# A two-layer transformer block on one core: the triangular inverse's lowest level in compact buffers on four quadrants, and the first layer's slot in a new order

## The chip, the cores and the metric

One Trainium2 chip, one of its cores. The metric is the device time of one launch in microseconds (us), median of three runs.

## The reference

`x` is (8, 256, 128) in float32. Four blocks are added to it in turn, each on a layer norm of `x`:

```python
x = x + L0_attn(_layernorm(x))   # gated delta rule, 16 heads, key 64, value 128
x = x + L0_ffn(_layernorm(x))    # x @ sign(weight).T
x = x + L1_attn(_layernorm(x))   # causal softmax attention, 16 heads of 8, 4 KV heads
x = x + L1_ffn(_layernorm(x))    # mixture of 8 experts, top 2
```

The change is in the first of them. q, k and v are projected, put through a causal convolution of four taps and silu, q and k are scaled to length one, and for each head

```python
def step(S, inp):
    q_t, k_t, v_t, a_t, b_t = inp
    kS = einsum('bhd,bhdv->bhv', k_t, S)
    kkS = einsum('bhd,bhv->bhdv', k_t, kS)
    S = a_t * (S - b_t * kkS) + einsum('bhd,bhv->bhdv', k_t, v_t)
    return (S, einsum('bhdv,bhd->bhv', S, q_t))
```

runs over 256 time steps. Its outputs are divided by their root mean square and projected.

## The kernel before

The recurrence is done in chunks of 128 time steps: within a chunk a unit triangular matrix of 128 x 128 has to be inverted, and the rest is matmuls. The work is cut into 32 units `n` (4 pairs of batch rows, 8 pairs of heads each: `NP`, `NG`); a unit has 8 half-chunk blocks of 64 x 64 to invert (`NJ`).

All engines run one loop over slots `s`, written out by hand for each engine. In slot `s` the unit `g = s - 9` is at its Gram matrices and masks, `i = g - 1` at the start of its inverse, `j = g - 2` at the inverse's end and the solves, `w = g - 3` at its output. An engine runs what stands in its list in that order, and waits on semaphores; a late operation holds up all that stands behind it on its engine. `s` goes from 9 to 43; k and q projections for units ahead run in slots up to 31, and items of the second layer stand in the last slots. The second layer then has a loop of its own ("ticks").

What a unit goes through, in the order of its data:

- `kproj`, `kcopy`, `kconv`, `ksilu`, `ksq`, `ksel` and `vproj`, `vcopy`, `vconv`, `vsilu`, `vtr`, `vV`: projections on TensorE, copies and silu on ScalarE. A convolution's three taps are each a `scalar_tensor_tensor` on VectorE (L1463), each waiting for the tap before. There are twelve taps in a slot.
- `gram(n, 0..2)` on TensorE (L719) fills banks 3 and 1; ScalarE's `exp` makes the decay masks from exponents that SP loads from DRAM (`exponents`, L469) and GpSimd makes causal (`causal`, L1896); VectorE's `am(n, 0..5)` (L1532, L1535) multiplies the two into `AM`. GpSimd's `scaled` (L1888) makes the scaled keys that `gram` needs, from factors that SP spreads (`spread`, L480).
- `blocks(n)` on SP, released by `am(n, 5)`: four DMAs write the diagonal 32-blocks of `AM` to DRAM (L489), four read them back into `SU` with one row of matrix per partition range (L495).
- `substitute(n)` on GpSimd (L1872 to L1880): forward substitution inside 16 x 16 blocks, a memset and 28 dependent steps over the free dimension.
- `inv_0` on VectorE: turns `SU` (L1546), spreads it on the diagonal of `YP` (L1548), transposes into `XP` (L1553). Then level 0 joins 16-blocks to 32-blocks: `inv_a` (L746), `inv_p` (L1557), `inv_b` (L757), `inv_y` (L1563, L1566), on 64 x 64 tiles. Level 1 joins 32 to 64 by the same functions, and `inv_c`, `inv_n`, `inv_d`, `inv_o` join 64 to 128.
- `solve1`, `u1`, `solve2`, `solve3`, `u2`, `out`, `ot`, `squares`, `rms`, `wout`: solves, output, root mean square and the output projection, which VectorE adds into `X` (L1595).

At the change of each group of 8 units come `lengths` and `gates` (per-head scalars; SP moves them to DRAM by `factors`), and in fixed slots a layer norm or the sign-weight matmul of a finished part. `fill` are matmuls without use that keep TensorE busy.

## Time and profile before

| | us |
|---|---|
| median of 3 runs | 1286.54 (1285.4 to 1288.22) |
| the profiled execution | 1296.63 |
| its span, first to last instruction | 1294.8 |
| TensorE busy | 1147.9 (89%) |
| VectorE busy | 925.0 (71%) |
| ScalarE busy | 814.3 (63%) |
| GpSimd busy | 644.5 (50%) |

"Busy" is the union of an engine's instructions. In the rows a line is start, duration, engine, line of the kernel, operation, output<-inputs, shapes and count; in brackets the idle time ahead of it and what ended it. A float32 matmul shows as two records, with a weight load (PEld) for each. On SP only DMA issues show, and what stands there is the time that issuing took. The chain that ended last runs over TensorE for 60% of the span. A part of this chain says which engine worked at each moment; it does not say which order would have been faster.

### The profile page before, as it was taken

What the parts mean: (1) busy time and instruction counts of PE and PEld (TensorE: products, weight loads), DVE (VectorE), ACT (ScalarE), POOL (GpSimd) and SP (SyncE); (2) the same over time, 40 slices, a digit from 0 to 9 for tenths busy, and PEclk for the clock granted to TensorE, in tenths of its full rate; (3) what the DMA queues carried; (4) which work ended last, traced back from release to release, by engine and by line L of the source; (5) the groups of instructions that cost most, each with busy time, mean ns of one, the idle gap of its engine ahead of it and who ended that gap; (6) DMA issues with size and microseconds to landing.
All of it is one profiled execution on the core that took longest, in us unless ns stands there. A gap on an engine that the chain in (4) does not pass through costs nothing.

```text
span 1294.8 us, 32678 instructions
## 1 busy us (share of the span) xinstructions
PE 1147.9 (89%) x12540; PEld 842.7 (65%) x12540; DVE 925.0 (71%) x1785; ACT 814.3 (63%) x1462; POOL 644.5 (50%) x1192
## 2 busy tenths in 40 slices
PE   5779999999999999989999999998779887898991
PEld 1123677777767777767777777776555454798991
DVE  4757689988899989889976787776556658152232
ACT  5876787887888787898785666765243433333330
POOL 1015667767667776767774766674220102204314
PEclk9879699999999999999997999999889998899996
DMA  4012332221221122112212222240101011488982
GB/s 150 1 60 70 113 84 54 53 71 52 51 69 48 53 52 73 45 53 54 69 25 74 65 68 53 58 67 15 28 7 33 18 19 68 153 282 299 319 301 55
DMA packets 130106, 106.18 MB, mean 82 GB/s; under 512 B 59472, under 2 KB 116816, under 8 KB 129696
## 3 DMA queue, kind: packets, MB, share of 16 engines
q1 hardware_dynamic: 127904, 99.90, 27.1%
q0 software_dynamic: 2048, 4.20, 1.0%
q8 instruction: 100, 1.64, 0.5%
q14 instruction: 54, 0.44, 0.1%
HBM read 84.21 MB, written 15.73 MB: 77 GB/s over the span
## 4 chain that ended last, share of the span: by engine, by line
PE 60%; DVE 16%; issue 7%; ACT 7%; POOL 5%; DMA 2%; SPq 1%; POOLq 0%; DVEq 0%; ACTq 0%
PE pair L719 8%; PE bank L1015 6%; PE bank L757 4%; PE pair L683 3%; PE bank L1022 3%; PE bank L969 3%; PE bank L746 3%; PE pair L651 3%; PE bank L771 3%; PE bank L764 3%; DVE vc L1463 2%; PE bank L815 2%; PE bank L799 2%; PE bank L842 2%; DVE kc L1463 2%
## 5 line engine op out<-in xcount | busy, mean ns | idle before, releaser
L1880 POOL TENSOR_TENSOR SU<-SU 128x28 f32<-128x28 f32 (+6 forms) x448 | 197.4, 441 | 35.1
L1876 POOL TENSOR_TENSOR SU<-SU 128x28 f32<-128x28 f32 (+6 forms) x448 | 194.0, 433 | 35.3
L1463 DVE SCALAR_TENSOR_TENSOR vc<-vy,conv,vc 128x512 f32<-128x512 f32 x192 | 144.5, 753 | 6.0 <-ACT vc L1160 1.5
L1463 DVE SCALAR_TENSOR_TENSOR kc<-ky,conv,kc 128x512 f32<-128x512 f32 x162 | 127.0, 795 | 7.6 <-ACT kc L1134 5.1
L1776 DVE TENSOR_TENSOR vy<-bank,vc 128x512 f32<-128x512 f32 x46 | 31.8, 692 | 98.9 <-PE bank L1015 97.6
L719 PE MATMUL pair<-SM,KQ 64*128 64x128 f32 (+1 forms) x512 | 77.3, 380 | 23.0 <-DVE AM L1532 20.4
L1941 POOL TENSOR_TENSOR RR<-RR,nh 128x8 f32<-128x8 f32 x32 | 57.1, 1785 | 75.3 <-DVE RR L1583 72.3
L1855 POOL TENSOR_TENSOR st<-st,nh 128x4 f32<-128x4 f32 x16 | 16.6, 1040 | 146.8 <-DVE st L1439 110.1
L651 PE MATMUL pair<-xnT,WQ 128*128 128x512 f32 x128 | 76.3, 681 | 5.9 <-ACT qb L1134 5.1
L757 PEld LDWEIGHTS bank<-YP,PP 64*64 64x64 f32 x2048 | 66.6, 138 | 17.1 <-issue 12.7
L1532 DVE TENSOR_TENSOR AM<-pair,SM 128x512 f32<-128x512 f32 x76 | 48.9, 685 | 38.1 <-PE pair L719 34.9
L746 PE MATMUL bank<-XP,AM 64*64 64x32 f32 x2048 | 71.8, 220 | 2.5 <-DVE XP L1566 1.2
L757 PE MATMUL bank<-YP,PP 64*64 64x32 f32 x2048 | 73.8, 223 | 0.1
L683 PE MATMUL pair<-xnT,WQ 128*128 128x512 f32 x128 | 72.3, 648 | 1.0 <-DVE SM L1482 1.0
L1872 POOL MEMSET SU<- 128x32 f32 x32 | 5.0, 156 | 137.0 <-DMA SU<-scratch 137.0
L746 PEld LDWEIGHTS bank<-XP,AM 64*64 64x64 f32 x2048 | 64.7, 134 | 12.2 <-issue 6.4
L719 PEld LDWEIGHTS pair<-SM,KQ 64*128 64x128 f32 x512 | 40.8, 194 | 47.0 <-DVE AM L1532 40.1
L1015 PE MATMUL bank<-YF,AM 128*128 128x128 f32 x512 | 68.0, 279 | 0.0
L719 PE MATMUL pair<-KQ 64*128 64x128 f32 (+1 forms) x512 | 67.3, 341 | 0.0
L1888 POOL TENSOR_TENSOR SM<-KQ,SM 128x512 f32<-128x512 f32 x32 | 44.1, 1377 | 44.1 <-DMA SM<-fscr 44.1
L1929 POOL DMA_INDIRECT SU<-ys,PP x32 | 30.3, 948 | 71.5 <-DMA ys<-YF 60.3
L1546 DVE STREAM_TRANSPOSE PP<-SU 128x512 f32<-128x512 f32 x32 | 35.0, 1093 | 41.8 <-PE bank L771 40.6
(307 smaller groups left out, 3118.7 us busy)
## 6 DMA issues: line engine op xcount, KB each, us to landing
AM<-in_wex_dram SPq DMA_DIRECT2D x32, 768.0 KB, 5.1
SM<-dscr SPq DMA_DIRECT2D x58, 256.0 KB, 3.7
V<-in_wex_dram SPq DMA_DIRECT2D x14, 768.0 KB, 5.5
et<-dscr SPq DMA_DIRECT2D x38, 256.0 KB, 3.7
SM<-fscr SPq DMA_DIRECT2D x64, 128.0 KB, 2.9
scratch<-AM SPq DMA_DIRECT2D x128, 48.0 KB, 1.8
SU<-scratch SPq DMA_DIRECT2D x128, 32.0 KB
xs<-idle SPq DMA_DIRECT2D x2, 1472.0 KB, 9.7
```

The costliest lines, as they stand in the source:

```text
L651: e.matmul(kbank(t)[:, :], wqkv[:, ct * 128:(ct + 1) * 128], xT[:, p % 3, :], start=True, stop=True).then_inc(s_kproj, 1)
L683: e.matmul(vbank(v)[:, :], wqkv[:, ct * 128:(ct + 1) * 128], xT[:, (n // NG) % 3, :], start=True, stop=True).then_inc(s_vproj, 1)
L719: ins = e.matmul(bank[(3, 1)[hh]][:, part], KQ[hp:hp + 64, m, b, 0, s0:s0 + 128], moved, start=True, stop=True)
L746: ins = e.matmul(half(bank[4][pq, j * 64:j * 64 + 64], lv, 0), block_of(n, j, q, 64 * q), half(XP[pq, j, :], lv, 0), start=True, stop=True)
L757: ins = e.matmul(half(bank[5][pq, j * 64:j * 64 + 64], lv, 1), PP[pq, j, :], half(YP[pq, j, :], lv, 1), start=True, stop=True)
L1015: ins = e.matmul(bank[4 if kind == "G" else 6][:, jj * 128:(jj + 1) * 128], W[:, o + jj * 128:o + jj * 128 + 128], XST[i % 2], start=True, ...
L1463: e.scalar_tensor_tensor(c, y[:, :, k:k + 256], conv[:, ct, k:k + 1], c, ALU.mult, ALU.add).then_inc(s_c, 1)
L1532: ins = e.tensor_tensor(AM[:, hh, part, :].rearrange("p (c n) -> p c n", c=3)[:, 0:3:2, :], G[:, :].rearrange("p (k t) -> p k t", k=2), E. ...
L1876: e.tensor_tensor(tmp[:, :, 0:k, 0:15 - k], sub[:, :, 0:k, k:k + 1].to_broadcast([128, 2, k, 15 - k]), sub[:, :, k:k + 1, k + 1:16].to_bro ...
L1880: e.tensor_tensor(sub[:, :, 0:k, k + 1:16], sub[:, :, 0:k, k + 1:16], tmp[:, :, 0:k, 0:15 - k], ALU.subtract).then_inc(s_su, 1)
L1888: e.tensor_tensor(KT2[:, n % 2], KQ[:, n % RK, :, 0, :], FB[:, n % 2, :].rearrange("p (b t) -> p b t", b=2), ALU.mult).then_inc(s_kt, 1)
L1941: e.tensor_tensor(RR[:, 1, :, :], RR[:, 0, :, :], nh[:, :].rearrange("p (t h) -> p t h", t=4), ALU.pow).then_inc(s_r2, 1)
```

## The change

- **Compact level 0.** New buffers `Y0`, `X0`, `PP0` (8 x 32 per partition). Level 0 works on 32 x 32 tiles at the four diagonal positions: `inv_a0`, `inv_b0` have 32 matmuls each with 16 columns, where 16 matmuls had 64 x 64 weights and 32 columns. VectorE's `inv_turn`, `inv_y0`, `inv_x0`, `inv_p0`, `inv_s0` handle half or a quarter of the elements; a new `inv_w0` widens `Y0` into `YP`, and `inv_x1` transposes that.
- **Substitution on 64 partitions.** `SU` shrinks from 1056 to 512 columns. The two 16-blocks that lay side by side in a partition now lie in partitions 8 apart, so each GpSimd step has half the elements. `blocks` reads back with eight DMAs of half the size, where there were four. The `SU` read-back waits for the turn of the unit before, which now stands before `am(4)`.
- **Taps of two tiles apart.** Each parity of k and v tiles has its own tap semaphore, and other work stands between a tile's taps.
- **A new order of the slot** on all engines. `exp` of unit `g + 1` runs at the end of slot `g`; `causal(g + 1)` moves to the head of GpSimd's slot; level 1's `inv_a1` moves to the end of the slot before; `rms` is cut in two. At the change of a group SP sends exponents' factors first, and `key_factors` and `spread` stand behind `blocks`.
- `inv_n` writes `XP`, `inv_c` writes bank 5; some `fill` and some semaphores go; the second layer's `GB` moves from `SU` into `V`.

```diff
-        SU = sb("SU", [128, 1056])
+        SU = sb("SU", [128, 512])
+        su2 = SU[:, :].rearrange("p (r x t) -> p r x t", r=16, x=2)
+        sub, tmp = su2[:, :, 0, :], su2[:, :, 1, :]
...
                 if n:
-                    e.wait_ge(s_tt, n)
+                    e.wait_ge(s_i0, 3 * n - 2)
                 for a in range(4):
                     e.wait_ge(s_bo[a], 16 * n + 16)
-                    e.dma_start(SU[32 * a:32 * a + 8, 0:1024], scratch[a].rearrange("(m c) r t -> m c (r t)", c=3)[:, 0:2, :]).then_inc(s_bi, 16)
+                    rows = scratch[a].rearrange("(m c) r t -> m c (r t)", c=3)
+                    for h in range(2):
+                        e.dma_start(SU[32 * a + 8 * h:32 * a + 8 * h + 8, 0:496], rows[:, 0:2, 528 * h:528 * h + 496]).then_inc(s_bi, 16)
...
             for n in range(NN):
-                if n and n + 1 < NN: spread(n + 1)
+                new = (n + 1) % NG == 0
+                if n and n + 1 < NN and not new: spread(n + 1)
                 if n + 1 < NN: exponents(n + 1)
                 blocks(n)
+                if n + 1 < NN and new:
+                    key_factors((n + 1) // NG)
+                    spread(n + 1)
...
+            def inv_a0(n):
+                if n:
+                    e.wait_ge(s_ip, 2 * n)
+                e.wait_ge(s_ix, 2 * n + 1)
+                for j in range(NJ):
+                    for a in range(4):
+                        r = slice(32 * a, 32 * a + 32)
+                        ins = e.matmul(bank[4][r, 16 * j:16 * j + 16], N4(n)[r, j // 2, j % 2, r], X0[r, j, 0:16], start=True, stop=True)
+                ins.then_inc(s_ia, 1)
...
+            def inv_turn(n):
+                if n:
+                    e.wait_ge(s_ib, 2 * n)
+                e.wait_ge(s_su, NSU * n + NSU)
+                e.transpose(flat(PP[:, :, :]).rearrange("p (t m) -> p t m", t=16),
+                            sub.rearrange("p r t -> p t r").unsqueeze(2).to_broadcast([128, 16, 2, 16])).then_inc(s_i0, 1)
...
-                    e.tensor_tensor(tmp[:, :, 0:k, 0:15 - k], sub[:, :, 0:k, k:k + 1].to_broadcast([128, 2, k, 15 - k]),
-                                    sub[:, :, k:k + 1, k + 1:16].to_broadcast([128, 2, k, 15 - k]), ALU.mult).then_inc(s_su, 1)
+                    e.tensor_tensor(tmp[:, 0:k, 0:15 - k], sub[:, 0:k, k:k + 1].to_broadcast([128, k, 15 - k]),
+                                    sub[:, k:k + 1, k + 1:16].to_broadcast([128, k, 15 - k]), ALU.mult).then_inc(s_su, 1)
...
                 if w >= 0:
...
                 if gap(s + 1, "norm") is not None:
                     norm(gap(s + 1, "norm"))
-                if g + 1 < NN: causal(g + 1)
                 if g < NN: substitute(g)
```

The order on VectorE in the middle of a slot with gates, before (L1546 is the turn of `SU`; L1535 is `am(4)` and `am(5)`; L1463 are taps):

```order
L1463 SCALAR_TENSOR_TENSOR kc<-ky,conv,kc 128x512 [waits s_kconv]
L1532 TENSOR_TENSOR AM<-pair,SM 128x2x256 [waits s_gk,s_exp] x2
L1563 TENSOR_TENSOR YP<-YP,bank 128x8x32 [waits s_ib]
L1569 STREAM_TRANSPOSE XP<-YP 32x8x32 [waits s_iy]
L1579 STREAM_TRANSPOSE ST<-bank 128x256 [waits s_ms]
L1583 SCALAR_TENSOR_TENSOR RR<-ST,QN 128x8 [waits s_r2,s_mt]
L1535 TENSOR_TENSOR AM<-pair,et 128x2x256 [waits s_gk,s_exp] x2
L1463 SCALAR_TENSOR_TENSOR kc<-ky,conv,kc 128x512 [waits s_kconv]
L1481 TENSOR_SCALAR SM<-pair,SM 80x512 [waits s_gab]
L1482 COPY SM<-pair 16x512
L1546 STREAM_TRANSPOSE PP<-SU 128x512 [waits s_su,s_yfc,s_yfd]
L1548 TENSOR_TENSOR YP<-PP,bmask 128x512 [waits s_tt]
```

and after (L1573 is the turn, L1564 are `am(4)` and `am(5)`, L1578 and L1584 `inv_y0` and `inv_x0`):

```order
L1627 STREAM_TRANSPOSE ST<-bank 128x256 [waits s_ms]
L1491 SCALAR_TENSOR_TENSOR vc<-vy,conv,vc 128x512 [waits s_vconv0]
L1561 TENSOR_TENSOR AM<-pair,SM 128x2x256 [waits s_gk,s_exp] x2
L1491 SCALAR_TENSOR_TENSOR vc<-vy,conv,vc 128x512 [waits s_vconv0]
L1573 STREAM_TRANSPOSE PP<-SU 128x512 [waits s_su,s_ib]
L1564 TENSOR_TENSOR AM<-pair,et 128x2x256 [waits s_gk,s_exp]
L1578 TENSOR_TENSOR Y<-PP,bmask 128x256 [waits s_i0]
L1564 TENSOR_TENSOR AM<-pair,et 128x2x256 [waits s_gk,s_exp]
L1584 STREAM_TRANSPOSE X<-Y 128x256 [waits s_i0]
L1633 SCALAR_TENSOR_TENSOR RR<-ST,QN 128x8 [waits s_r2,s_mt]
L1491 SCALAR_TENSOR_TENSOR vc<-vy,conv,vc 128x512 [waits s_vtap,s_vcopy]
L1588 TENSOR_SCALAR PP<-bank,bmask 128x8x16 [waits s_ia]
```

The turn stood behind the last `am` and now stands before its last two.

The order on SP at the change of a group, before (L446 and L448 are `factors`, L480 `spread`, L469 `exponents`, L489 and L495 `blocks`):

```order
L446 DMA dscr<-SM 16x512 [waits s_gs]
L448 DMA fscr<-SM 16x512 [waits s_fr]
L480 DMA SM<-fscr 64x512 [waits s_kt,s_fw]
L480 DMA SM<-fscr 64x512
L469 DMA et<-dscr 128x2x256 [waits s_mk,s_am,s_fw]
L469 DMA SM<-dscr 128x2x256 [waits s_mk,s_am]
L469 DMA SM<-dscr 128x4x128 [waits s_mk,s_am]
L489 DMA scratch<-AM 32x12x32 [waits s_bi,s_am]
L489 DMA scratch<-AM 32x12x32 x3
L495 DMA SU<-scratch 8x1x1024 [waits s_bo0,s_tt]
L495 DMA SU<-scratch 8x1x1024 [waits s_bo1]
```

and after (L453 is `key_factors`, L485 `spread`, L494 and L502 `blocks`):

```order
L494 DMA scratch<-AM 32x12x32 [waits s_bi,s_am]
L494 DMA scratch<-AM 32x12x32 x3
L502 DMA SU<-scratch 8x1x496 [waits s_bo0,s_i0]
L502 DMA SU<-scratch 8x1x496
L502 DMA SU<-scratch 8x1x496 [waits s_bo1]
L502 DMA SU<-scratch 8x1x496
L502 DMA SU<-scratch 8x1x496 [waits s_bo2]
L502 DMA SU<-scratch 8x1x496
L502 DMA SU<-scratch 8x1x496 [waits s_bo3]
L502 DMA SU<-scratch 8x1x496
L453 DMA fscr<-SM 16x512 [waits s_fr]
L485 DMA SM<-fscr 64x512 [waits s_kt,s_fw]
```

`spread` stood ahead of `exponents` and `blocks`, and now stands behind both; `blocks` has eight reads.

The order on TensorE around level 0, before (L746 is `inv_a`, L651 `kproj`, L791 and L799 `solve2` and `solve3`, L842 `wout`):

```order
L791 MATMUL bank<-U,AM 128x128 [waits s_u1]
L791 MATMUL bank<-U,AM 128x128 x3
L746 MATMUL bank<-XP,AM 64x2x16 [waits s_ix,s_x]
L746 MATMUL bank<-XP,AM 64x2x16 x15
L651 MATMUL pair<-xnT,WQ 128x512 [waits s_vtap]
L799 MATMUL bank<-V,YF 128x128 [waits s_v2]
```

and after (L756 and L764 are `inv_a0` and `inv_b0`, L665 `kproj`, L819 `solve2`):

```order
L756 MATMUL bank<-X,AM 32x16 [waits s_ix,s_ip]
L756 MATMUL bank<-X,AM 32x16 x31
L819 MATMUL bank<-U,AM 128x128 [waits s_u1]
L819 MATMUL bank<-U,AM 128x128 x3
L665 MATMUL pair<-xnT,WQ 128x512 [waits s_vtap]
L764 MATMUL bank<-Y,PP 32x16 [waits s_ip]
L764 MATMUL bank<-Y,PP 32x16 x31
```

Level 0 has twice the matmuls at a quarter of the area, and its first group stands before `solve2`.

## Rows read from the trace of the kernel before

**Rows 1.** The page, busy time and granted clock in 40 slices.

```profile
PE 1147.9 (89%) x12540; PEld 842.7 (65%) x12540; DVE 925.0 (71%) x1785; ACT 814.3 (63%) x1462; POOL 644.5 (50%) x1192
...
PEclk9879699999999999999997999999889998899996
```

**Rows 2.** Busy us of PE, PEld, DVE, ACT, POOL by stretch; PEclk, DMA.

```profile
166.80:674.70 507.90, 489.49 (x5632) 371.35 (x5632) 464.47 (x842) 419.26 (x748) 360.43 (x678) 0.99 0.21 55
674.70:705.70 31.00, 30.25 (x294) 23.91 (x290) 17.82 (x34) 16.62 (x30) 16.04 (x37) 0.78 0.27 72
705.70:873.20 167.50, 155.03 (x1920) 124.50 (x1918) 131.83 (x266) 113.01 (x207) 115.43 (x243) 1.00 0.27 62
...
679.40:693.00 13.60, 13.60 (x102) 10.03 (x100) 6.82 (x13) 4.70 (x10) 4.30 (x6) 0.50 0.37 92
```

**Rows 3.** Timeline of TensorE, start and duration in us, two slots.

```profile
471.23 0.49 PE L719 MATMUL pair<-SM,KQ 64*128 64x256 f32 x2
...
498.53 0.70 PE L719 MATMUL pair<-SM,KQ 64*128 64x256 f32 x4
...
501.16 0.70 PE L719 MATMUL pair<-SM,KQ 64*128 64x256 f32 x4 [0.90 <-DVE AM L1532]
...
503.27 0.64 PE L826 MATMUL bank<-qb,ones 128*32 128x256 f32 x8
...
513.89 1.12 PE L746 MATMUL bank<-XP,AM 64*64 64x32 f32 x32
514.95 1.12 PE L651 MATMUL pair<-xnT,WQ 128*128 128x512 f32 x2
...
523.14 0.70 PE L719 MATMUL pair<-SM,KQ 64*128 64x256 f32 x4
```

**Rows 4.** Timeline of VectorE in the same slot.

```profile
505.12 1.29 DVE L1535 TENSOR_TENSOR AM<-pair,SM 128x512 f32<-128x512 f32 x2
...
508.24 1.11 DVE L1546 STREAM_TRANSPOSE PP<-SU 128x512 f32<-128x512 f32 x1 [1.17 <-PE bank L771]
509.39 1.06 DVE L1548 TENSOR_TENSOR YP<-PP,bmask 128x512 f32<-128x512 f32 x1
510.48 0.71 DVE L1553 STREAM_TRANSPOSE XP<-YP 128x512 f32<-128x512 f32 x1
...
512.12 2.32 DVE L1463 SCALAR_TENSOR_TENSOR vc<-vy,conv,vc 128x512 f32<-128x512 f32 x3
...
515.06 0.69 DVE L1557 TENSOR_TENSOR PP<-bank,lmask 128x512 f32<-128x512 f32 x1
...
526.23 0.74 DVE L1463 SCALAR_TENSOR_TENSOR kc<-ky,conv,kc 128x512 f32<-128x512 f32 x1
```

**Rows 5.** Timeline of GpSimd, one substitution.

```profile
514.05 0.16 POOL L1872 MEMSET SU<- 128x32 f32 x1 [4.55 <-DMA SU<-scratch]
514.29 0.25 POOL L1876 TENSOR_TENSOR SU<-SU 128x28 f32<-128x28 f32 x1
...
521.90 0.76 POOL L1880 TENSOR_TENSOR SU<-SU 128x112 f32<-128x112 f32 x1
...
523.54 0.42 POOL L1880 TENSOR_TENSOR SU<-SU 128x112 f32<-128x112 f32 x1
...
529.12 0.23 POOL L1880 TENSOR_TENSOR SU<-SU 128x28 f32<-128x28 f32 x1
```

**Rows 6.** Timeline of SP, DMA issues of the same unit.

```profile
506.44 1.87 SPq L489 DMA_DIRECT2D scratch<-AM  x4
509.38 2.65 SPq L495 DMA_DIRECT2D SU<-scratch  x4
```

**Rows 7.** Timeline of GpSimd, a substitution in a slot without k taps.

```profile
769.41 0.15 POOL L1872 MEMSET SU<- 128x32 f32 x1 [4.69 <-DMA SU<-scratch]
...
782.29 0.23 POOL L1880 TENSOR_TENSOR SU<-SU 128x28 f32<-128x28 f32 x1
```

**Rows 8.** The page, DMA issues: count, KB each, median us to landing.

```profile
SM<-fscr SPq DMA_DIRECT2D x64, 128.0 KB, 2.9
```

More of the change, by code:

```diff
@@ L238, in wide @@
             return b[:, :].rearrange("p (j n) -> p j n", j=NJ)
-        def mask(lv, q):
-            return lmask[q, lv:lv + 1, :].to_broadcast([q.stop - q.start, NJ, 64])
         def N4(n):
@@ L569, in _ @@
             exponents(0)
+            key_factors(0)
             spread(0)
@@ L1062, in _ @@
                 if has_g: gram(g, 0)
+                if has_g: vproj(2 * g)
                 if gap(s, "lengths") is not None: lengths(gap(s, "lengths"))
@@ L1100, in _ @@
                 more(s, 7)
-                if has_w and has_g: wout(w, 1)
-                elif w < 0: fill(2)
-                if has_i: inv_b(i, 0)
+                if has_w: wout(w, 0)
+                if has_w: wout(w, 1)
+                elif w < 0: fill(4)
+                for it in PREP0.get(s, []): prep(*it)
                 if has_j: out(j, 0)
@@ L1106, in _ @@
                 more(s, 8)
-                if has_j: out(j, 1)
-                if has_g: vtr(2 * g)
+                if has_i: inv_a1(i)
+                if has_j and j >= NN - 3: out(j, 1)
                 more(s, 9)
@@ L1279, in _ @@
             e.activation(sgn[:, :], sgn[:, :], ACT.Sign).then_inc(s_sgn, 1)
-            e.wait_ge(s_zero, 3)
+            e.wait_ge(s_zero, 4)
+            for i in range(3):
+                exp(0, i)
             def item(kind, *a):
@@ L1374, in _ @@
-                more(s, 1)
-                if 0 < g < NN: vV(2 * g - 1)
-                if has_g: exp(g, 2)
-                if gap(s, "norm") is not None: norm(gap(s, "norm"))
-                more(s, 2)
-                more(s, 3)
-                if has_k: ksilu(2 * s)
+                has_n = 0 <= g and g + 1 < NN
+                if s % NG == 3 and 1 <= s // NG < NP: gates1(s // NG)
+                if has_l: lengths1(p)
+                if s % NG == 4 and 1 <= s // NG < NP: gates2(s // NG)
@@ L1389, in _ @@
-                if has_k: ksq(2 * s + 1)
-                if has_g: vcopy(2 * g)
+                more(s, 0)
+                if has_k: ksq(2 * s)
+                if has_g: vcopy(2 * g)
+                if gap(s, "norm") is not None: norm(gap(s, "norm"))
+                if has_j: inv_yf(j)
+                more(s, 1)
+                more(s, 2)
+                if has_j: inv_n(j)
+                more(s, 3)
+                if has_k: ksilu(2 * s + 1)
+                if has_k: ksq(2 * s + 1)
```

342 lines of the change are left out of this document (183 added, 159 removed).

## Prediction

> **What bounds the kernel now.** I read the busy shares and slices first, then the stages, then one slot on each engine. TensorE is busy for 89% of the span and no other engine is above 71% [rows 1]. The stage that the change rewrites is the first layer's slot loop: 20 slots from 166.8 to 674.7 us (25.4 us each), one slot of 31 us, and seven slots without k projections from 705.7 to 873.2 us (23.9 us each) [rows 2]. In an ordinary slot of the first kind the first `gram` matmuls start at 498.53 and again at 523.14 us: 24.61 us, in which TensorE has one pause, 0.90 us before the second `gram`, for VectorE's `am` [rows 3]. The other 23.7 us are matmuls back to back, so TensorE sets these slots. VectorE, ScalarE and GpSimd wait for it; GpSimd stands idle 4.55 us a slot for the blocks of `SU` [rows 5]. What lies before 166.8 us and behind 873.2 us is hardly touched, and I take it as it is.
>
> **TensorE's part of the change.** Level 0 of the inverse had two groups of 16 matmuls, 32 records, at 1.12 us each [rows 3]; start to start they are 1.05 us. They become 32 matmuls of 32 rows and 16 columns, 64 records, on four quadrants. As 16 rounds of one record per quadrant, the old group takes 66 ns a round for two quadrants. The halved width takes a round to 33 ns, if width decides it; `squares`, the one group that uses four tiles of the array side by side, has 8 records in 0.64 us, two rounds of 256 columns each, so a third and fourth tile can overlap [rows 3]. I add 10 ns a round for them: 16 x 43 ns, 0.7 us. The other end is a price per record: 33 ns times 64 is 2.1 us. I take 0.65 to 0.7, so 0.8 us a slot is saved on both groups; at the other end 2.1 us a slot is lost. The 0.90 us pause goes too, since `vproj` and `inv_c` now stand between the `gram`s. TensorE alone would need 23.7 - 0.8 = 22.9 us a slot.
>
> The Trainium skill has a rule for each end. "TensorE: Matmul & The Clock Gate", section on packing small matmuls, lets tiles start a few ns apart; "TensorEngine Tiling (Array Packing)", section Instruction Overhead, advises against tiling a dimension that is already small, since a matmul has an overhead of about 60 cycles. By the first the group would take 0.7 us or less, by the second, if the overhead is paid by every record, about 1.6 us as an estimate; no row here shows a 16-column matmul on four quadrants.
>
> **VectorE's part.** Old level 0 was a turn 1.11, a spread 1.06, a transpose 0.71 and a mask 0.69 [rows 4], with a subtraction behind. New: the turn again, a spread and a transpose of half the elements (0.55 and 0.4 by halving), a mask of a quarter (0.2), a subtraction of half, and a widening that I bound by 0.7 and 1.06, the rows of its size; 0 to 0.6 us less. Three taps that follow each other take 2.32 us, 0.77 each, against 0.74 for one alone, and one with unrelated work behind it gives the engine back about 0.1 us earlier [rows 4]; six such pairs, 0.6 us. VectorE gets about 1 us a slot freer. It doesn't bound a slot, so this is worth nothing by itself.
>
> **What comes in its place: the substitution's loop.** The order on VectorE is what matters. Before, `am(5)` stood ahead of the turn of `SU` within a slot, so a substitution had a whole slot and more to reach the turn. Now the turn stands before `am(4)` and `am(5)`. `am(5)` releases the blocks' DMAs, these the substitution, this the next slot's turn, and the turn the next `am(5)`: a closed loop of one slot. Its length, term by term:
> 1. Turn to the end of `am(5)`: turn 1.05, `am(4)` 0.6, the spread 0.55, `am(5)` 0.65: 2.85 us [rows 4].
> 2. `am(5)` to the blocks in `SU`. Four scratch DMAs issue over 1.9 us, then, before, four `SU` DMAs over 2.65 us, 0.66 each; the first had to wait until 509.38 us for the turn [rows 6]. That wait goes, but eight DMAs are now issued, one after the other on SP. The eighth starts at 2.0 + 7 x 0.66 = 6.6 us. The last of the old four started at 509.38 + 3 x 0.69 = 511.44, and GpSimd went on at 514.05 [rows 5, 6]: 2.6 us. Together 9.2 us. Halved transfers may land 0.3 sooner, and dearer issues may add 0.5.
> 3. The substitution. From 514.05 to 529.35 us it takes 15.3 us beside the slot's taps; in a slot without k taps 769.41 to 782.52, 13.1 us [rows 5, 7]. A step of 28 elements takes 0.25 us and one of 112 takes 0.42, but 0.76 when taps run [rows 5]: 0.002 us an element. All 28 steps have 2240 elements, and now 1120, so 2.2 us come off; the step's fixed part stays. That leaves 13.1 us, and one tap fewer stands in its window. Nine taps lay in it before and four without k, so a tap costs (15.3 - 13.1) / 5 = 0.4 us: 12.6 us. Without k taps 13.1 - 2.2 = 10.9 us.
> Sum: 24.65 us a slot with k taps, 22.95 without. This is above TensorE's 22.9, and I also walked the new order from one turn to the next over TensorE, ScalarE and VectorE with the durations of these rows: the other way round comes to 23 us. So the substitution's loop sets the slot, and most of what TensorE saves becomes waiting in front of the turn.
>
> **The slots with extra work.** Lengths, gates, norms and signed matmuls add 1 to 3 us of TensorE to some slots now; against a loop of 24.65 they fit into the new slack except where they exceed it. At each start of a new group of eight, SP now issues `key_factors` and `spread` behind the blocks. GpSimd's `scaled` needs them and stands ahead of `substitute`: the SP queue is 7.2 us past `am(5)`, the factors take about 2 us to DRAM, `spread` 0.6 + 2.9 us to land [rows 8], `scaled` 1.3. The substitution starts 4.9 us late, with fewer taps beside it (-0.8): 28.8 us for that slot, where such a slot now takes 498.53 - 471.23 = 27.3 us [rows 3].
>
> **The sum**, against this execution's span of 1294.8 us:
> - 20 slots: 18 x 24.65 + 2 x 28.8 + 0.6 for gates = 501.9 against 507.9 us: -6.
> - seven slots: 7 x 22.95 = 160.6 against 167.5 us: -7.
> - the 31 us slot: two effects, late `scaled` and the clock. TensorE was granted the lower of its two levels, 1.2 of 2.4 GHz, from 679.4 to 693 us [rows 2], in the slot in which `lengths` runs. The new order can meet it or not. I take -2.
> - ramp, turn-over and second layer: 0, +-4.
> That is -15 us, 1279.8 us of span. The execution lasted 10 us longer than the median of the timed runs, 1286.5; the difference carries over: **1271 us**, -1.2%. The loop's terms are good to +-0.8 us a slot in all (0.3 down to 0.5 up for the DMAs, 0.4 either way for the substitution), so this case reaches from 1256 to 1284 us.
>
> **Rivals.**
> - *The loop is short, TensorE bounds.* If taps hinder the smaller steps less, and DMAs issue at 0.5 us, the loop is 22.9 and TensorE and the walk give 23.2 to 23.5 us with extras: 18 x 23.5 + 2 x 28 = 479, seven slots at 22: 154; -29 - 13 - 2 = -44: 1242 us, 1235 to 1256. For it: the two-tile steps had four-dimensional patterns that are simpler now. Against: every term of the loop above would have to be at its low end. Chance 0.2.
> - *The loop is longer, slower.* The same loop decides the other way from 25.4 us a slot. With 0.8 us on every DMA issue, or a tap that costs a short step as much as 0.6 us (small steps leave more gaps to be caught in), it is 25.8: 18 x 25.8 + 2 x 30.5 = 525, +17; the seven slots -1: +16, 1303 us. For it: the single tap that meets a step stretches it by 0.5 us and more. Against: eight DMAs of half the size. Chance 0.12.
> - *Four quadrants cost by the record.* 2.1 us a group: TensorE 23.7 + 2.1 = 25.8 a slot, 25.9 with extras: 18 x 25.9 + 2 x 29.5 = 525, +17; seven slots without the removed fills and within the loop: -6, sum +9 with the turn-over: 1296 us. This is where the Trainium skill's instruction overhead would lead ("TensorEngine Tiling (Array Packing)"). Against it: 33 ns a record already held with 64-wide weights. Chance 0.08.
> - *A wait inside the loop.* `am(4)` needs `gram(2)`, this stands behind `inv_d`, and `inv_d` waits for ScalarE's `inv_n` behind `vcopy` and `inv_yf`. In my walk `gram(2)` is done 1 us before `am(4)` wants it. If ScalarE runs late by 1.6 us there (in the slots with gates it has 2.6 us more to do), the loop gets 0.6 us longer: 25 slots x 0.6 = +15: 1286 us, 1282 to 1293. Chance 0.1.
>
> **Numbers.** The forecast case has 0.5. The range from 1246 to 1292 us leaves out the lower half of the short loop and the slow cases' upper parts, about 0.2. A measurement of this kernel can tell about 0.2% (2.6 us) from no change. Faster by more: 0.46 of the forecast case, 0.2 and 0.02, 0.68; within: 0.04 of it, 0.05 of the last rival and 0.01, 0.1; slower: 0.22.
>
> **What would show it.** Right: GpSimd's substitution of about 12.6 us, ending right before the turn, the turn idle for `SU` in most slots, TensorE with 1 to 2 us of pauses a slot, and groups of 0.7 us at level 0. Wrong: the turn never waits for GpSimd (short loop), groups of 2 us with no pause (records), or slots over 25.4 us. Half-clock stretches that come or go, each about 6 us as at 679.4 us, can shift the total by that much without any of these reasons.

## The result: slower by 0.85%, and where the time is

The changed kernel took 1300.49 us (median of 20 runs, 1293.12 to 1311.13), the kernel before 1288.12 us (20 runs). The ratio is 1.0085, with a 95% interval of 1.006 to 1.0109. The forecast was 1271 us, with a range of 1246 to 1292. The time lies outside the range, and it moved the other way.

From the page of the changed kernel: busy time, granted clock and the chain of work that ended last. They answer to [rows 1].

```profile
PE 1132.5 (87%) x14560; PEld 817.2 (63%) x14560; DVE 895.9 (69%) x1817; ACT 803.8 (62%) x1456; POOL 562.1 (43%) x1193
...
PEclk9879899989999989999988998999789888899996
...
PE 31%; POOL 21%; issue 14%; SPq 12%; DVE 10%; DMA 8%; ACT 3%; POOLq 0%; DVEq 0%; ACTq 0%
```

Every engine works less than before: TensorE 1132.5 us against 1147.9, VectorE 895.9 against 925.0, GpSimd 562.1 against 644.5. Yet the span grew. In the chain TensorE has fallen to 31%, where it had 60% before, and GpSimd, SyncE's queue and DMAs have 41%: this is the substitution's loop that the prediction described.

The same loop can be followed. Timelines of the changed kernel in one ordinary slot, first VectorE, then SyncE, two taps on VectorE, GpSimd and TensorE (start, duration, line; L1573 is the turn, L1491 are taps, L1564 `am(4)` and `am(5)`, L756 and L764 the two level-0 groups):

```profile
379.34 1.09 DVE L1573 STREAM_TRANSPOSE PP<-SU 128x512 f32<-128x512 f32 x1 [2.12 <-POOL SU L1942]
380.35 0.65 DVE L1564 TENSOR_TENSOR AM<-pair,SM 128x512 f32<-128x512 f32 x1
380.91 0.59 DVE L1578 TENSOR_TENSOR Y<-PP,bmask 128x256 f32<-128x256 f32 x1
381.43 0.67 DVE L1564 TENSOR_TENSOR AM<-pair,SM 128x512 f32<-128x512 f32 x1
...
404.01 1.09 DVE L1573 STREAM_TRANSPOSE PP<-SU 128x512 f32<-128x512 f32 x1 [2.12 <-POOL SU L1942]
```

```profile
382.13 1.87 SPq L494 DMA_DIRECT2D scratch<-AM  x4
384.10 5.21 SPq L502 DMA_DIRECT2D SU<-scratch  x8
```

```profile
390.94 1.41 DVE L1491 SCALAR_TENSOR_TENSOR kc<-ky,conv,kc 128x512 f32<-128x512 f32 x2
```

```profile
390.80 0.12 POOL L1934 MEMSET SU<- 128x16 f32 x1 [2.30 <-DMA SU<-scratch]
391.01 0.76 POOL L1938 TENSOR_TENSOR SU<-SU 128x14 f32<-128x14 f32 x1
...
403.69 0.21 POOL L1942 TENSOR_TENSOR SU<-SU 128x14 f32<-128x14 f32 x1
```

```profile
381.05 1.12 PE L665 MATMUL pair<-xnT,WQ 128*128 128x512 f32 x2 [0.57 <-DVE AM L1564]
382.60 0.72 PE L756 MATMUL bank<-X,AM 32*32 32x16 f32 x64 [0.42 <-DVE X L1584]
...
385.20 0.80 PE L764 MATMUL bank<-Y,PP 32*32 32x16 f32 x64
```

From turn to turn it is 404.01 - 379.34 = 24.67 us (24.65 forecast). The turn waited 2.12 us for GpSimd's last step at 403.69. Term by term: turn to the end of `am(5)` 2.76 us (2.85), from there to the memset 8.70 (9.2), the substitution from there to the next turn 13.21 (12.6, plus 0.1 to the turn). The level-0 groups take 0.72 and 0.80 us, 0.65 to 0.73 from start to start (0.65 to 0.7).

So in this slot the mechanism and the length are as forecast. To see where the total went, I compare two traces taken on one chip by the first pair of experiments below, the kernel before unchanged and the changed kernel unchanged. The columns are the stretch, its length, then busy us (and instructions) of PE, PEld, DVE, ACT and POOL, the granted clock, the DMA share and GB/s. The stretches are: first `gram` to the fourth, the 20 slots, the slot behind them, the seven slots without k tiles, the drain (last tile's `gram` to the last output product), and the rest. First the kernel before, then the changed one:

```profile
92.70:160.20 67.50, 58.64 (x501) 32.22 (x500) 49.06 (x70) 51.73 (x91) 43.50 (x88) 0.95 0.38 103
160.20:669.70 509.50, 491.08 (x5634) 372.58 (x5634) 464.72 (x842) 419.56 (x748) 364.50 (x686) 0.99 0.22 56
669.70:696.30 26.60, 25.70 (x292) 20.44 (x290) 17.66 (x34) 16.61 (x30) 14.78 (x34) 0.94 0.34 84
696.30:863.70 167.40, 154.98 (x1919) 124.46 (x1918) 131.94 (x266) 113.02 (x207) 116.64 (x244) 1.00 0.27 62
863.70:960.30 96.60, 75.14 (x777) 55.92 (x776) 54.05 (x112) 40.40 (x72) 31.50 (x59) 0.91 0.10 17
960.30:1285.20 324.90, 268.93 (x3263) 213.46 (x3261) 149.79 (x354) 108.12 (x214) 69.87 (x72) 0.90 0.48 154
```

```profile
93.40:164.60 71.20, 58.04 (x655) 32.24 (x655) 49.41 (x74) 55.37 (x99) 29.59 (x81) 0.95 0.28 72
164.60:674.00 509.40, 483.98 (x6914) 355.77 (x6910) 441.54 (x861) 410.77 (x742) 313.35 (x688) 0.98 0.23 60
674.00:701.00 27.00, 25.41 (x353) 21.25 (x350) 16.77 (x35) 16.25 (x30) 10.56 (x26) 0.87 0.29 78
701.00:866.60 165.60, 151.37 (x2354) 122.64 (x2352) 128.04 (x273) 111.61 (x207) 104.53 (x251) 0.97 0.28 63
866.60:971.90 105.30, 83.28 (x881) 58.22 (x879) 54.21 (x118) 37.41 (x65) 30.18 (x65) 0.80 0.10 16
971.90:1296.60 324.70, 267.71 (x3253) 212.26 (x3251) 148.02 (x349) 106.98 (x213) 70.17 (x72) 0.89 0.47 154
```

| stretch | before | changed | forecast of the difference | measured |
|---|---|---|---|---|
| up to the fourth `gram` | 160.2 | 164.6 | 0 | +4.4 |
| 20 slots | 509.5 | 509.4 | -6 | -0.1 |
| slot behind them | 26.6 | 27.0 | -2 | +0.4 |
| seven slots | 167.4 | 165.6 | -7 | -1.8 |
| drain | 96.6 | 105.3 | 0 (with the rest, +-4) | +8.7 |
| rest | 324.9 | 324.7 | 0 | -0.2 |

The slots gained 1.5 us where 15 were forecast, and the two ends of the pipeline, for which the forecast had no working at all, lost 13 us.

One execution is one sample. The two behind this table took 1286.97 and 1298.50 us. In the first pair of traces (1296.63 and 1299.64 us) the slots show the same: 507.9 and 510.7 us, then 31.0 and 27.8, then 167.5 and 167.8, together 0.1 us less. The drain grew there too, from 96.4 to 102.0 us. But the stretch from the first `gram` to the fourth did not grow; the kernel before had 27 us at half clock in it, and the changed one 16:

```profile
92.30:166.80 74.50, 67.55 (x500) 37.96 (x500) 49.99 (x70) 51.99 (x91) 45.68 (x97) 0.82 0.37 103
```

```profile
93.20:164.70 71.50, 61.20 (x656) 34.06 (x656) 49.24 (x74) 55.34 (x99) 29.04 (x80) 0.89 0.26 67
```

So the missing gain of the slots, 13.5 to 15 us, and the longer drain, 5.6 to 8.7 us, show in both pairs. The longer start shows in one of them only.

### The profile page after: what moved, and what is told of

Same layout as the page of the kernel before. It is cut to its first block, busy times and chain, and to the rows that moved or that the text cites. A ratio compares the mean times of both kernels' runs of the same rounds, so it can differ in the third digit from the quotient of the medians.

```text
span 1297.8 us, 36909 instructions
## 1 busy us (share of the span) xinstructions
PE 1132.5 (87%) x14560; PEld 817.2 (63%) x14560; DVE 895.9 (69%) x1817; ACT 803.8 (62%) x1456; POOL 562.1 (43%) x1193
## 4 chain that ended last, share of the span: by engine, by line
PE 31%; POOL 21%; issue 14%; SPq 12%; DVE 10%; DMA 8%; ACT 3%; POOLq 0%; DVEq 0%; ACTq 0%
POOL SU L1938 9%; POOL SU L1942 9%; SPq L502 7%; PE bank L1045 5%; DMA SU<-scratch 4%; PE bank L999 3%; PE bank L1052 3%; SPq L494 3%; DMA scratch<-AM 1%; DVE AM L1564 1%; PE pair L733 1%; DVE Y L1578 1%; PE pair L957 1%; PE pair L972 1%; PE bank L827 1%
## 5 line engine op out<-in xcount | busy, mean ns | idle before, releaser
L1938 POOL TENSOR_TENSOR SU<-SU 128x14 f32<-128x14 f32 (+6 forms) x448 | 153.7, 343 | 35.1
L1942 POOL TENSOR_TENSOR SU<-SU 128x14 f32<-128x14 f32 (+6 forms) x448 | 149.1, 333 | 35.1
L1491 DVE SCALAR_TENSOR_TENSOR vc<-vy,conv,vc 128x512 f32<-128x512 f32 x192 | 152.5, 794 | 15.6 <-ACT vc L1186 15.3
L1491 DVE SCALAR_TENSOR_TENSOR kc<-ky,conv,kc 128x512 f32<-128x512 f32 x162 | 123.7, 784 | 10.0 <-ACT kc L1160 8.3
L2004 POOL TENSOR_TENSOR RR<-RR,nh 128x8 f32<-128x8 f32 x32 | 65.2, 2038 | 107.1 <-DVE RR L1633 107.0
L665 PE MATMUL pair<-xnT,WQ 128*128 128x512 f32 x128 | 74.1, 665 | 14.9 <-DVE AM L1564 9.1
L1916 POOL TENSOR_TENSOR st<-st,nh 128x4 f32<-128x4 f32 x16 | 18.4, 1153 | 146.9 <-DVE st L1467 109.9
L1789 DVE TENSOR_REDUCE SM<-pair 128x4 f32<-128x1024 f32 x32 | 39.1, 1221 | 39.8 <-PE pair L957 39.6
L1181 ACT ACTIVATE vy<-pair 128x512 f32<-128x512 f32 x64 | 38.3, 599 | 44.4 <-PE pair L697 43.6
L1934 POOL MEMSET SU<- 128x16 f32 x32 | 4.0, 127 | 141.8 <-DMA SU<-scratch 141.8
L1045 PEld LDWEIGHTS bank<-YF,AM 128*128 128x128 f32 x512 | 63.9, 196 | 0.0
L1991 POOL DMA_INDIRECT V<-ys,PP x32 | 30.3, 947 | 71.2 <-DMA ys<-YF 56.3
L1573 DVE STREAM_TRANSPOSE PP<-SU 128x512 f32<-128x512 f32 x32 | 34.7, 1085 | 37.3 <-POOL SU L1942 37.3
L1561 DVE TENSOR_TENSOR AM<-pair,SM 128x512 f32<-128x512 f32 x76 | 48.6, 680 | 16.9 <-PE pair L733 12.6
L1276 ACT ACTIVATE qb<-pair 128x512 f32<-128x512 f32 x29 | 17.3, 597 | 69.4 <-PE pair L845 69.4
## 6 DMA issues: line engine op xcount, KB each, us to landing
SU<-scratch SPq DMA_DIRECT2D x256, 15.5 KB
```

What stands on the lines that cost most here:

```text
L665: e.matmul(kbank(t)[:, :], wqkv[:, ct * 128:(ct + 1) * 128], xT[:, p % 3, :], start=True, stop=True).then_inc(s_kproj, 1)
L1045: ins = e.matmul(bank[4 if kind == "G" else 6][:, jj * 128:(jj + 1) * 128], W[:, o + jj * 128:o + jj * 128 + 128], XST[i % 2], start=True, ...
L1491: e.scalar_tensor_tensor(c, y[:, :, k:k + 256], conv[:, ct, k:k + 1], c, ALU.mult, ALU.add).then_inc(s_c, 1)
L1561: ins = e.tensor_tensor(AM[:, hh, part, :].rearrange("p (c n) -> p c n", c=3)[:, 0:3:2, :], G[:, :].rearrange("p (k t) -> p k t", k=2), E. ...
L1789: e.tensor_reduce(MX[ch][:, x, 1, :, 2 * u - 2:2 * u], D2[ch][:, :].rearrange("p (g m t) -> p g m t", g=2, m=2), AX.X, ALU.max).then_inc(s ...
L1938: e.tensor_tensor(tmp[:, 0:k, 0:15 - k], sub[:, 0:k, k:k + 1].to_broadcast([128, k, 15 - k]), sub[:, k:k + 1, k + 1:16].to_broadcast([128, ...
```

## Experiments

### Two kernels unchanged, on one chip

The profiled execution of before that the forecast rested on had a span of 1294.8 us, above the median of its runs. These two runs give both traces on one chip.

> The kernel before, unchanged, so that its trace and the traces of the next three runs are of one chip. The profiled execution of before that the forecast started from took 1296.6 us while the median of its runs was 1288.1. Theory: that execution was an untypical one, with more half-clock time of TensorE than most; this trace should then show the 20 slots from gram(3) to gram(23) at 508 us again (within 2), because they held only 6.8 us at half clock, and the slot behind gram(23) at 25 to 27 us where the earlier trace had 30.9 with 13.7 us at half clock. Rival: the long slot belongs to the kernel (31 us again).

Measured: 1291.72 us (10 runs), ratio to before 1.003 (0.9995 to 1.0066), which is the same kernel against itself; the trace's span is 1285.2 us. The 20 slots take 509.5 us and the slot behind them 26.6, with 3.4 us at half clock. The 31 us slot of [rows 2] was a half-clock stretch of that one execution, not a property of the kernel. So the theory holds. Its runs also show what goes with one kernel's time: 1285.3 us at a mean granted clock of 0.952, 1302.5 us at 0.936.

> The changed kernel, unchanged, on the same chip. Both theories: 0.6 to 1.2% over before. Stages: 510 us for the 20 slots, ordinary turn-to-turn times of 24.5 to 24.9 us (the closed loop). If the loop decides, the 20 slots are within 2 us of 510.7 whatever the half-clock time is; if half-clock time decides, they move with it by half its difference from 27 us.

Measured: 1307.46 us (5 runs), ratio 1.0128 (1.0086 to 1.0171). The 20 slots took 509.4 us with 23.9 us at half clock, against 510.7 with 27.3 in the first trace: too alike to tell the two theories apart.

### Opening the loop (on another chip)

The next four ran together on a chip where the kernel before took 1326.6 us; the stretch behind the output products is some 35 us longer there, so only the slots are compared with the traces above. The first edit puts both last mask products ahead of the turn:

```diff
                 if has_g: vconv(2 * g, 2)
-                if has_i: inv_turn(i)
                 if has_g: am(g, 4)
-                if has_i: inv_y0(i)
                 if has_g: am(g, 5)
+                if has_i: inv_turn(i)
+                if has_i: inv_y0(i)
                 if has_i: inv_x0(i)
```

> The changed kernel with one thing moved: on VectorE am(4) and am(5) stand before the turn of SU, as they did before the change; nothing else. Theory A (the substitution's loop sets the slot, 24.67 us from turn to turn): the loop is open, since am(5) no longer waits for the turn; a slot falls to 23.2 to 23.6 us, the slots at a change of group to some 26, the whole by 20 x 1.2 + 3 x 3 + 7 x 1 = 40 us, to 1260 +- 10 us. Rival B (another way round, over ScalarE and VectorE, is as long): slots stay over 24.3 us, 1293 to 1300 us. Rival C (the added half-clock stretches are the loss): slots with full clock hardly change, 1290 to 1300 us.

Measured: ratio 1.0104 (1.0072 to 1.0137). The loop did open: ordinary slots fell from 24.67 us to between 23.3 and 24.9, and the 20 slots to 502.7 us. The total did not fall below the changed kernel's ratios (1.0085, 1.0128; it did not run on this chip), so theory A's 1260 us was missed. The slot behind the 20 took 31.9 us, 20.5 of them at half clock, and the seven slots 174.1 us, since without k tiles TensorE waits about 2.1 us in each for the transposed blocks, which now come later.

The second edit takes the group change apart: the factors of the next group are written and spread between the scratch writes and the block reads, and the length factors' exponential goes ahead of the mask's.

```diff
+                if between is not None: spread(between)
                 if n:
                     e.wait_ge(s_i0, 3 * n - 2)
...
-                if has_n: exp(g + 1, 0)
                 if has_l: lengths2(p)
+                if has_n: exp(g + 1, 0)
```

> The changed kernel with the change of group mended alone: ScalarE makes the key factors before exp, SP writes them before the blocks and issues spread between the blocks' writes and reads, so scaled no longer stands waiting before the substitution. Theory A: the slot of 28.8 us at each change of group falls to 25.8, three times: -9 us, 1291 +- 4 us, ordinary slots stay at 24.67. Rival B and C: within 3 us of 1300.

Measured: ratio 1.0047 (1.0016 to 1.0078); the slot behind the 20 took 24.0 us, but the 20 slots stayed at 508.7, with 34 us at half clock. What this edit removes can be read in the changed kernel at a group change, on SyncE, GpSimd and VectorE:

```profile
486.74 5.12 SPq L502 DMA_DIRECT2D SU<-scratch  x8
491.96 0.38 SPq L453 DMA_DIRECT2D fscr<-SM  x1
493.62 2.42 SPq L485 DMA_DIRECT2D SM<-fscr  x4
```

```profile
497.06 1.27 POOL L1950 TENSOR_TENSOR SM<-KQ,SM 128x512 f32<-128x512 f32 x1 [9.76 <-DMA SM<-fscr]
498.28 0.12 POOL L1934 MEMSET SU<- 128x16 f32 x1
```

```profile
478.46 1.29 DVE L1561 TENSOR_TENSOR AM<-pair,SM 128x512 f32<-128x512 f32 x2 [2.55 <-PE pair L733]
...
480.75 1.07 DVE L1573 STREAM_TRANSPOSE PP<-SU 128x512 f32<-128x512 f32 x1
...
509.59 1.06 DVE L1573 STREAM_TRANSPOSE PP<-SU 128x512 f32<-128x512 f32 x1 [3.92 <-POOL SU L1942]
```

GpSimd stood 9.76 us for the factors, with the substitution behind `scaled`, and the slot came to 509.59 - 480.75 = 28.84 us, as forecast (28.8). But the turn at 480.75 had itself come late. It did not wait for GpSimd: VectorE had lost 2.55 us to `gram` matmuls in a stretch at half clock. This makes a second long slot per group, 27.3 us, that the forecast had not counted.

Both edits together:

> Both of the edits: am(4) and am(5) before the turn, and spread early. Theory A: with the loop open the late spread matters little, so 0 to 5 us below the first of them: 1255 to 1260 us. Rival B: 1285 to 1295 us.

Measured: ratio 1.009 (1.0061 to 1.0119), 20 slots at 495.8 us, seven slots at 174.2. Together they give 14 us in the 20 slots, and the total shows none of it. The seven slots take back 9 us of it. For the rest the stages can't be added up, since the traced execution took 1325.3 us, 13 less than the median.

The last of the four leaves out the last seven of the substitution's 14 rounds, and so part of the inverse:

```diff
-                for k in range(14, 0, -1):
+                for k in range(14, 7, -1):
```

> The changed kernel, its order untouched, with the last seven of the substitution's fourteen rounds left out (14 of 28 steps; the inverse is incomplete). Theory A: the substitution falls from 12.5 to about 6.5 us, the loop to 18.5 us, and something else sets the slot at 23 to 23.5 us: 1260 +- 10 us, as with the am first. Rival B: no change over 5 us.

Measured: ratio 0.9869 (0.9831 to 0.9907); 20 slots at 481.9 us, busy time of PE, PEld, DVE, ACT, POOL:

```profile
163.60:645.50 481.90, 474.82 (x6914) 351.57 (x6910) 442.22 (x861) 409.94 (x742) 224.25 (x411) 0.99 0.24 64
```

TensorE now idles only 7 us in 482. GpSimd did nothing else differently, so what the loop held back in the changed kernel's 20 slots is 509.4 - 481.9 = 27.5 us (across two chips): 18 us of idle time, and 9 us of busy time that went with half-clock stretches, 10 us of them here against 24. TensorE's own bound with this work is about 23.7 us a slot, where the forecast had 22.9.

### Pauses and the clock

In the first trace of the changed kernel TensorE falls to half clock seven times in the slots. Five times it had just paused, for 1.4 to 3.6 us; other pauses of 2.1 to 2.3 us were followed by no drop. A slot without k tiles shows such a pause, and the last line below a stretch behind one of 3.58 us (PEclk 0.50):

```profile
737.63 1.06 PE L811 MATMUL bank<-V,YF 128*128 128x128 f32 x8
740.95 0.71 PE L756 MATMUL bank<-X,AM 32*32 32x16 f32 x64 [2.26 <-DVE X L1584]
```

```profile
702.80:713.00 10.20, 9.84 (x43) 5.42 (x44) 3.82 (x7) 2.90 (x5) 8.08 (x29) 0.50 0.21 64
```

The change had also removed a filler of four matmuls from these slots. This edit puts fillers into the pauses:

```diff
+                if g > 0 and g % NG == 0 and has_p: fill(8)
                 if has_p: kproj(2 * s + 2)
+                elif has_g: fill(8, s < 36)
                 if has_i: inv_a0(i)
```

> The changed kernel with filler matmuls in the pauses of TensorE: 1.7 us of them ahead of the first level-0 group in each slot that has no k tiles (where TensorE waits 0.9 to 2.3 us for the transposed diagonal blocks), and ahead of the first k projection in the slot behind a group change (where it waits 2.2 us). Theory A (the drops to half clock in these slots follow those pauses, and cost): the half-clock time from gram(24) to gram(31) falls from 17 us to under 5, the seven slots from 168 to 162 or less, and the whole is 5 to 9 us faster than the changed kernel. Theory B (the closed loop sets those slots and the clock there costs nothing): seven slots within 2 us of 168, the whole within 2 us. Theory C (the fills only add work): slower by up to 1.7 us for each of 9 slots, 5 to 15 us in all.

Measured: 1300.15 us (10 runs), ratio 1.0066 (1.0035 to 1.0098). The median is 7 us below the changed kernel's beside it, but the intervals of the two ratios overlap (1.0086 to 1.0171) and the two traced executions differ by 1.3 us, so a gain is not shown. The seven slots took 165.9 us, the same as without fillers, though their half-clock time fell from 10.2 to 3.4 us. That is what theory B said of them, and the turn of `SU` waited for GpSimd in six of the seven.

The same fillers with both edits that open the loop:

> Both edits that open the loop (the last two products of the mask ahead of the turn; the key factors spread ahead of the block reads, the group-change exponentials behind) with the same filler matmuls. Theory A: the 20 slots at 490 to 498 us as with both edits alone (495.8), the seven slots from 174 to 163 or less, the whole 10 to 16 us faster than the changed kernel on this chip, and so a little faster than before. Theory B: the seven slots stay at 172 to 176, since there the turn has only been put later; the whole within 3 us of the changed kernel.

Measured: 1285.55 us (12 runs), ratio 0.9952 (0.9922 to 0.9982). On one chip and with the same fillers, the two edits that open the loop are worth 14.6 us: 498.5 against 510.4 us in the 20 slots. Theory A had 10 to 16 us below the changed kernel, and it is 22. The seven slots took 164.6 us, 1 us less than with the loop closed, although no turn waited for GpSimd any more: there something else comes next. So the closed loop, group changes included, costs about 1.1% of the time, and this can be seen once TensorE does not lose it again in pauses. The run was repeated beside the next two:

> The kernel of g2_open_fills again, on the chip of the next two. 0.3 to 0.7% faster than before, as there (0.9952); 20 slots 497 to 500 us.

Measured: 1286.78 us (12 runs), ratio 0.9953 (0.9925 to 0.9982), as expected; 496.6 us for the 20 slots. Now fillers in the drain as well, in three pauses:

```diff
+                if s == 42: fill(6, False)
                 if has_j: inv_b1(j)
...
+                if s == 41: fill(16, False, 4)
                 if has_j: solve1(j)
...
+                if s == 42: fill(5, False, 4)
                 if has_w: wout(w, 0)
```

> The same with fillers in the drain too: 3.5 us of them ahead of the first solve of the slot that ends the inversions, 1.3 and 1.1 us ahead of the level-1 product and of the output product of the next slot, where TensorE waited 4.9, 1.8 and 2.0 us. Theory A (the drain, from gram(31) to the last output product, is longer than before's 96.6 us because TensorE falls to half clock in its pauses: 32 to 42 us of it at half clock against 17): half-clock time there falls by 10 us or more, and the whole is 3 to 6 us faster than without them. Theory B (the drain is longer because the last tile now needs 68 us from its turn to its output product against 53): the half-clock time may fall, but the drain stays within 2 us of 101, the whole within 2 us.

Measured: 1275.80 us (6 runs), ratio 0.9865 (0.983 to 0.99), 11 us less. The drain without and with these fillers:

```profile
863.20:964.50 101.30, 80.63 (x911) 58.17 (x910) 54.21 (x118) 37.33 (x65) 28.38 (x60) 0.85 0.10 16
```

```profile
859.70:951.30 91.60, 75.47 (x1022) 56.16 (x1018) 54.03 (x118) 37.09 (x65) 28.42 (x60) 1.00 0.11 18
```

TensorE is given 108 more matmuls and is busy 5 us less, since the granted clock goes from 0.85 to 1.00. The drain gets 9.7 us shorter, shorter even than before's 96.6. Theory A had asked for 3 to 6 us and got more. So in this kernel the drain was long because its pauses took the clock away. The changed kernel's own drain (105.3 us at 0.80) was not run with these fillers; its trace has pauses of 4.3 and 1.8 us at the same operations and half-clock stretches of 14 and 21 us behind them, where this kernel without fillers had 4.9 and 1.8, and 10 and 21.

### The new inverse without the new order

One part of the change alone: the compact inverse, its substitution on 64 partitions and its eight block reads, in the order of the kernel before on all engines (some semaphores, the bank of `inv_c` and the place of `GB` stay as in the changed kernel). TensorE's loop, inverse calls only:

```diff
-                if has_j: inv_b1(j)
+                if has_j: inv_a1(j)
...
+                if has_g: gram(g, 1)
+                if has_j: inv_b1(j)
...
+                if has_i: inv_a0(i)
                 if has_p: kproj(2 * s + 3)
+                elif has_g and s < 36: fill(4)
...
+                if has_i: inv_b0(i)
...
-                if has_i: inv_a1(i)
```

> One part of the change alone: the inverse's 32-blocks in compact buffers on four quadrants with the substitution on 64 partitions and eight block reads, in the slot order of the kernel before on all five engines (turn and diagonal blocks behind the mask's products, level-1 product in the next slot, taps of a tile together, mask exponentials in their own slot, key factors spread ahead of the blocks). Theory A (that order is bound by TensorE, 60% of before's chain, and the compact groups take 0.35 us less each): 0.7 us less in each of 27 slots, ramp and drain as before: 20 slots at 494 to 498 us against 508 to 510, the whole 1.2 to 1.6% faster than before. So the new slot order, not the new inverse, is what costs, 2 to 2.5%. Theory B (the four more block reads on SyncE, 2.6 us, and the longer way to the substitution put the closed loop at the end of these slots too): 20 slots at 506 us or more, the whole within 0.3% of before. Theory C: the compact groups cost TensorE as much as before elsewhere: PE-busy of the 20 slots not lower than 489 us.

Measured: 1273.05 us (6 runs), ratio 0.9876 (0.9836 to 0.9916). Its trace, whose execution at 1262.4 us is 10 us under that median, in the same stretches, and its chain:

```profile
93.50:159.70 66.20, 57.66 (x626) 31.38 (x627) 47.97 (x72) 51.74 (x91) 35.43 (x90) 0.94 0.37 97
159.70:659.80 500.10, 476.44 (x6912) 358.57 (x6912) 453.47 (x862) 417.08 (x748) 315.06 (x684) 0.99 0.22 59
659.80:683.80 24.00, 23.26 (x356) 18.69 (x352) 17.61 (x35) 16.57 (x30) 12.06 (x33) 1.00 0.37 94
683.80:841.20 157.40, 149.53 (x2368) 119.38 (x2364) 132.61 (x273) 112.70 (x207) 97.73 (x245) 1.00 0.29 66
841.20:934.50 93.30, 72.30 (x908) 53.93 (x904) 53.32 (x114) 40.24 (x72) 27.95 (x60) 0.91 0.11 17
```

```profile
PE 65%; DVE 10%; ACT 9%; issue 7%; POOL 4%; DMA 3%; SPq 2%; POOLq 0%; DVEq 0%; ACTq 0%
```

TensorE's busy time in the 20 slots fell from 491.1 to 476.4 us, 0.73 us a slot, which is what the level-0 groups were forecast to save. That is 14.7 us, of which 9.4 arrived: TensorE's idle time there grew from 18.4 to 23.7 us, its waits for `am` from 12.8 to 16.1. Every stretch of the first layer is shorter than before's, and SyncE's queue and GpSimd have 6% of the chain instead of 33%. Theory A holds, with the 20 slots 2 us above its bounds and the total at their edge. The changed kernel did not run on this chip; by its ratios on others, 1.0085 and 1.0128, the new slot order costs 2.1 to 2.6%, far outside the intervals. That is more than the new inverse gives.

A last run tried to use those pauses for `am`: the squares, 0.64 us, ahead of the second `gram`.

```diff
+                if has_w: squares(w)
                 if has_g: gram(g, 1)
                 if has_j: inv_b1(j)
                 elif j < 0: fill(4)
-                if has_w: squares(w)
```

> The inverse alone in the slot order of the kernel before, with one move on TensorE: the sums of squares of the tile three slots back (8 matmuls, 0.64 us) go ahead of the second Gram product instead of behind the level-1 product, since TensorE waited there for VectorE's mask products in 15 of 20 slots, 16.1 us in all. Theory A (with its loops open the order is bound by TensorE and by what it waits for there): about 0.6 us less in each of these slots, the 20 slots at 490 to 494 us against 500.1, the whole 1.6 to 2.2% faster than before. Theory B (the squares wait for ScalarE's copies there, or something else comes last in the slot): within 0.3% of the inverse alone, 0.985 to 0.991 of before.

Measured: 1284.37 us (12 runs), on another chip, ratio 0.9958 (0.9927 to 0.9989): slower than the inverse alone, so both theories missed in size. What TensorE waited for in the 20 slots (us in total, times, longest):

```profile
PE pair L731 <- DVE AM L1562: 11.7, 25, 1.0
PE bank L854 <- ACT V L1279: 7.8, 9, 2.9
```

```profile
159.70:678.20 518.50, 491.23 (x6916) 368.06 (x6912) 455.34 (x862) 417.29 (x747) 313.59 (x681) 0.96 0.21 56
```

The wait for `am` fell from 16.1 to 11.7 us, but the squares now wait 7.8 us for ScalarE's copies, up to 2.9 at a time, and 41 us of the 20 slots ran at half clock, against 10. Theory B had named this wait. Of the 18 us by which the 20 slots grew, 15 are busy time of TensorE for the same matmuls, so most of it is the clock; one of the half-clock stretches, 20 us long from 260.9 us, began without a pause ahead of it.

## Why the prediction was wrong

The loop that it described is there. Two steps failed: the sum over the slots, which gained 1.5 us instead of 15, and "ramp, turn-over and second layer: 0, +-4", which lost 13 us in one pair of traces and 3 in the other, the drain's 6 to 9 in both. By its own steps:

- **TensorE's part: the saving was right.** 0.72 and 0.80 us for groups expected at 0.65 to 0.7, and 0.73 us a slot less busy time, shown by the inverse alone. What was left, 22.9 us, was counted from one slot without extra work; over the 20 slots it is 23.7. The price per record (2.1 us a group) is out. The Trainium skill ("TensorEngine Tiling (Array Packing)", section Instruction Overhead) gives each matmul an overhead of about 60 cycles; paid by every record in turn, it would be 1.6 us a group, as an estimate. The measurement decides against that reading: 64 records start within 0.65 to 0.73 us, so records on different quadrants overlap.
- **The loop: right.** 24.67 us against 24.65, each term within 0.6 us. Without k tiles a substitution takes 10.4 to 11.1 us (10.9 forecast), and four of the seven slots measured 22.4 to 22.7 us (22.95).
- **The sum of the 20 slots: 7.5 us too low** (501.9 against 509.4). The turns of the second trace give 398.0 us for the 16 slots outside the group changes, 24.87 each, 3.6 us more than forecast. Each group change has two long slots instead of one, 57.0 and 54.7 us a pair where 53.5 were put down: 4.8 us. (The 0.6 us put down for gates are in these.) The forecast walked the factors' way to the substitution and was right on it (28.84); it did not walk the slot ahead, in which a half-clock stretch makes `gram` late for VectorE. The kernel before has such a stretch at the same places (263.5 and 468.3 us in its second trace), and this was its one long slot, 28.0 and 29.6 us from turn to turn, with 24.6 behind it. The forecast put the 28.8 us in the place of this slot, but they came behind it.
- **The seven slots: 5 us too low.** Three of them are 23.1 to 26.1 us long. TensorE pauses up to 2.3 us for the transposed blocks there, and half-clock stretches follow some of the pauses. The forecast saw that fillers went, but took it as work saved. Fillers in these pauses took most of the half-clock time away and left the stretch at 165.9 us, so the clock is not shown to be the cause here; what else made the three slots long stays open.
- **"Ramp, turn-over and second layer: 0, +-4": 13 us in the table, 3 in the first pair of traces.** It had no row behind it. The drain is +8.7 us (+5.6 in the first pair), with 42 us at half clock against 17, and the fillers there point to the clock. The first slots are +3.7, in this pair alone: TensorE waited for the value tiles' transposes (first line, changed kernel) where before it waited for other things for less:

```profile
PE pair L708 <- ACT vc L1190: 6.1, 4, 3.1
```

  In the kernel before that wait was 0.3 us. The `silu` it needs now stands behind other work of ScalarE. This was read, not tried by a run of its own.
- **The 31 us slot, -2: a term without a basis.** The kernel before has 26.6 us there in its other execution, and the changed kernel 27.0 and 27.8.
- **The step from span to median: right for a reason not given.** The forecast subtracted the profiled execution's surplus of 8 to 10 us over the median without saying what it was. It was half-clock time of that execution: the same kernel's other trace has a span of 1285.2 us at a clock of 0.952, against 1294.8 at 0.942, and 7.0 us of the difference lie between the first `gram` and the fourth. Taking it off leads to a typical execution of the kernel before, so this step is no part of the miss. Against the kernel before, the forecast was 15.5 us less and the result 12.4 us more, 27.9 us apart; the rows of the table above, forecast against measured, hold 26.4 of them.
- **The rivals.** None had the right reason. The two that gave 1296 and 1303 us, and the wait inside the loop at 1286, all made the ordinary slot longer. It did not get longer. What was missing is a case in which the slots are as forecast and the clock and the ends take the gain back, although the last paragraph had named a half-clock stretch as worth 6 us each. Summed over the trace the changed kernel had 185 and 182 us at half clock in its two traces, the kernel before 151 and 124.

What stays open: whether the fillers in the slots alone give anything, what made the first slots longer in one pair of traces, and what part each of the order's other moves (mask exponentials a slot ahead, taps of two tiles apart) has in the 2.1 to 2.6%.

The inverse alone in the old order (1273.05 us) and the opened loop with all fillers (1275.80 us) were both faster than the kernel before on their chip (1289.89 us).

## What to carry to other kernels

An order that takes work off the bounding engine can put a closed loop over slower engines around each slot: sum that loop before the saving, and open it before filling. Walk the first and last slots and the group changes as carefully as the steady slot, since pauses there are larger, and in the drain here they cost more than their length. Try the cheaper operation in the old order first: here this was the whole gain.
